# A fused cross-attention and expert kernel: weighted sums placed one step behind their scores

## The reference

```python
def attention(queries, keys, values):
    q = heads(queries @ Wq + bq); k = heads(keys @ Wk + bk); v = heads(values @ Wv + bv)
    scores = jnp.einsum('bhqd,bhkd->bhqk', q, k) / jnp.sqrt(jnp.float32(dh))
    attn = jax.nn.softmax(scores, axis=-1)
    ctx = jnp.einsum('bhqk,bhkd->bhqd', attn, v)
    return ctx.transpose(0, 2, 1, 3).reshape(B, L, D) @ Wo + bo

x = x + jnp.tanh(g_xattn[0]) * attention(_layernorm(x), ctx_1024, ctx_1024)
x = x + jnp.tanh(g_ffn[0]) * _moe(_layernorm(x))      # top 2 of 8 experts, relu between W1 and W2
```

## Time and profile before

| | us |
|---|---|
| median of 3 runs | 815.17 |
| lowest and highest run | 811.1 and 815.72 |
| the profiled execution | 809.99 |
| its span, first to last instruction | 807.8 |
| mean granted TensorE clock | 0.979 of full speed |

### The profile page before, as it was taken

How to read it: one execution, slowest core, us unless ns; L and a number is a source line. 1 busy time by engine, 2 the same in 40 slices (tenths; PEclk the granted TensorE clock), 3 DMA queues, 4 the chain that set the end, 5 groups by cost and what they waited for, 6 DMA issues and landing times.

```text
span 807.8 us, 21024 instructions
## 1 busy us (share of the span) xinstructions
PE 716.0 (89%) x6536; PEld 482.1 (60%) x6537; DVE 604.7 (75%) x1256; ACT 404.1 (50%) x783; POOL 460.3 (57%) x453
## 2 busy tenths in 40 slices
PE   3678999888887888877799999999999999999993
PEld 2344555454544445433477777777777777777771
DVE  5767888988889988887577877667666666776663
ACT  3266777677776776666533233333333333333330
POOL 6224544666566665544767767765565665655533
PEclk9799999999999999997999999999999999999997
DMA  6536655777677656653343323343323333222322
GB/s 185 135 107 196 198 160 181 173 183 191 140 188 187 172 135 188 161 158 100 87 110 49 53 48 50 52 56 46 46 47 52 53 46 47 46 49 41 53 34 27
DMA packets 96798, 85.45 MB, mean 106 GB/s; under 512 B 22256, under 2 KB 86000, under 8 KB 96592
## 3 DMA queue, kind: packets, MB, share of 16 engines
q1 hardware_dynamic: 80752, 65.73, 30.7%
q0 software_dynamic: 15680, 18.69, 14.9%
q10 hardware_dynamic: 288, 0.00, 0.0%
HBM read 53.61 MB, written 30.62 MB: 104 GB/s over the span
## 4 chain that ended last, share of the span: by engine, by line
PE 63%; DVE 19%; issue 9%; ACT 4%; DMA 2%; POOL 1%; another core or an unknown queue 1%; SPq 1%; DVEq 0%; POOLq 0%; ACTq 0%
PE banks L1779 22%; PE banks L1764 8%; PE banks L1766 7%; PE banks L1765 7%; DVE negmax L1127 6%; PE banks L1680 4%; PE banks L1590 3%; ACT probs L935 2%; PE banks L1668 2%; PE banks L1576 2%; PE banks L1750 2%; PE banks L1723 2%; DVE stats L1051 2%; PE banks L1640 1%; PE banks L1627 1%
## 5 line engine op out<-in xcount | busy, mean ns | idle before, releaser
L998 ACT ACTIVATE hid<-banks,b_col 128x256 f32<-128x256 f32 (+1 forms) x312 | 122.7, 453 | 200.9 <-DVE hl L1469 95.8
L1779 PE MATMUL banks<-wall,hh 128*128 x568 | 205.1, 381 | 2.6 <-DVE hl L1469 2.6
L787 POOL DMA_INDIRECT out_dram<-yb,dest_idx x71 | 125.5, 1767 | 121.1 <-DVE yb L1524 109.4
L1127 DVE TENSOR_REDUCE negmax<-banks 128x4 f32<-128x1024 f32 x128 | 155.6, 1217 | 21.1 <-PE banks L1640 20.8
L935 ACT ACTIVATE probs<-banks 128x1024 f32<-128x1024 f32 x128 | 130.9, 1024 | 69.0 <-PE banks L1668 66.0
L1764 PE MATMUL banks<-xh,wall 128*128 128x256 f16 (+1 forms) x624 | 161.3, 263 | 3.3 <-issue 2.4
L1765 PE MATMUL banks<-xl,wall 128*128 128x256 f16 (+1 forms) x624 | 161.2, 263 | 0.0
L1766 PE MATMUL banks<-xh,wall 128*128 128x256 f16 (+1 forms) x624 | 161.2, 263 | 0.0
L1779 PE MATMUL banks<-wall,hl 128*128 x568 | 144.9, 274 | 0.0
L1680 PE MATMUL banks<-probs,vaug 128*32 128x256 f32 x1024 | 83.6, 398 | 26.1 <-ACT probs L935 17.0
L709 POOL DMA_INDIRECT token_lists<-entry,place_i x64 | 69.4, 1084 | 61.1 <-ACT probs L935 41.3
(11 more groups left out here) (201 smaller groups left out, 1188.2 us busy)
## 6 DMA issues: line engine op xcount, KB each, us to landing
raw<-in_L_ffn_W SPq DMA_DIRECT2D x16, 512.0 KB, 6.3
wst<-in_L_ffn_W SPq DMA_DIRECT2D x16, 512.0 KB, 6.7
k_parts<-kparts SPq DMA_DIRECT2D x48, 128.0 KB
q_parts<-qparts SPq DMA_DIRECT2D x48, 128.0 KB
ks<-k_parts SPq DMA_DIRECT2D x64, 96.0 KB
qs<-q_parts SPq DMA_DIRECT2D x64, 96.0 KB
xin<-in_x SPq DMA_DIRECT2D x16, 256.0 KB, 2.8
cin<-in_ctx SPq DMA_DIRECT2D x16, 256.0 KB, 3.2
```

Of the source, the lines that this page charges most:

```text
L787: nc.gpsimd.indirect_dma_start(out_rows, bass.IndirectOffsetOnAxis(dest_idx[par][:, s:s + 1], 0), yb[par][:, s, :], None, compute_op=ALU.a ...
L998: ins = nc.scalar.activation(hid[half][:, c % (HC // 2), 0:subs(j) * P], banks[:, b, c % 2 * TS:c % 2 * TS + subs(j) * P], ACT.Relu, bias= ...
L1127: nc.vector.tensor_reduce(negmax[:, c, 8 * (g // 2):8 * (g // 2) + 8].rearrange("p (m g p2) -> p m g p2", m=2, g=2)[:, :, g % 2, :], banks ...
L1779: ins = nc.tensor.matmul(dst, h_[:, c, s * P:(s + 1) * P], w_, start=(c == 0 and k == 0), stop=(c == HC - 1 and k == 1))
```

## The change

On TensorE the weighted sum of step u-1 now stands in step u, behind that step's scores and maxima's scores. The weighted sum of step 7 stands in step 0 of the next body, behind its maxima's scores and ahead of the turned maxima, the k projection and the router. In the last body the weighted sums stay where they were, but for the eighth of batch 14, which comes there from the body before. On ScalarE the copy of the last group of sums moves with it, behind the first exponential of the next body. VectorE's, GpSimd's and SyncE's orders are the same.

```diff
-                def copy_out(g):
-                    n = m - 1
+                def copy_out(n, g):
                     act.wait_ge(av_mm, 8 * n + 2 * g + 2)
...
                         if v in (2, 4, 6):
-                            copy_out(v // 2 - 1)
+                            copy_out(m - 1, v // 2 - 1)
                     if v == 0:
+                        if post:
+                            copy_out(m - 2, 3)
                         if attention:
                             max_row(m - 1, 1)
...
-                if attention:
-                    copy_out(3)
+                if isinstance(m, int) and m == NB:
+                    copy_out(m - 1, 3)
...
                     if maxima:
                         scores_max(m, par, u)
+                    if u == 0 and post:
+                        attend(m - 2, par, 7)
+                    elif u > 0 and attention and not last:
+                        attend(m - 1, 1 - par, u - 1)
                     if u == 0:
                         if attention:
                             turn_max(m - 1, 1)
...
-                    if attention:
+                    if last:
                         attend(m - 1, 1 - par, u)
```

## The result

| | before | after |
|---|---|---|
| median, us (20 runs each) | 811.9 | 817.89 |
| lowest to highest | 808.52 to 815.72 | 814.2 to 821.29 |
| profiled execution: span, us | 807.8 | 815.8 |
| mean granted TensorE clock | 0.979 | 0.971 |

The ratio of after to before is 1.0068, with a 95% interval from 1.0054 to 1.0081: 0.7% or some 5.5 us slower, where 2.3 us faster was forecast. That is within 1%, but on the other side and clear of zero. The forecast counted from the three runs it was shown (815.17 us); over twenty runs the same kernel's median is 811.9, so the forecast gain would end at 809.6.

The account below looks back on a forecast made before the run. VectorE, 92% busy in mid-attention, was taken as the fuller engine, its router and maxima's-score waits the source of gain. Terms -0.5 - 1.4 - 0.2 + 0.15 - 0.35 = -2.3 us took 815.17 to 812.9; range 804 to 821.

Parts of the forecast that it names:

- The turns, in TensorE's queue: From one body to the next: eight turns gain 0.03 to 0.27 us each, four cost 0.21 to 0.31.
- The first bodies: Bodies 1 to 3, where VectorE truly waits for TensorE: gains of 0.5, 1.4 and 0.2 us.
- The waits: Before weighted sums near nothing; VectorE's for maxima's scores 11.7 to some 5 us, for the router 20.5 to some 25.
- the sum of the middle: Twelve turns of the attention part's long middle: gains of 0.93 against costs of 1.08, so it costs 0.15 us.
- the prediction's second kind of turn: Turns with a late reduction: turned maxima and logits come 0.31 us later; four such turns cost 1.08 together.
- The exponential's wait was the bound: Rival, TensorE's 21.7 us of waits before weighted sums: half back gives 804 us, nearly all 795; chance 0.15.
- The sum in the way at each turn: Rival, first step of a body: 0.57 us at 13 turns, net +5 us (820), or +11 (826); chance 0.20.
- The late gather: Rival, end of the attention part: GpSimd's late gather delays the experts, +3 us less 2.3, about 816; chance 0.05.
- Experts: Behind the attention part: they start 2 to 3 us sooner and keep their length.

Follow-up runs that it names:

- chip E: Fifth chip, one session: the changed kernel unedited, 0.9999 against the kernel before; with GpSimd's step 0 list scatter released one exponential later, 1.0016.
- chip A: One session: two versions with only part of the change, 1.0036 and 1.0024 against the kernel before; both kernels without list scatters, 798.51 before and 795.19 us after.
- the lag alone: Changed kernel with only weighted sums 1 to 7 moved, the eighth and ScalarE's last copy at the body's end as before: 1.0036 against the kernel before.
- eighth only: Kernel before with only the eighth weighted sum and its copy moved into the next body's first step: 1.0024 against the kernel before.
- chip D: One session: the changed kernel unedited, twice, 818.55 us (1.0079) and 815.97; with body 15 in the old order 1.0028; the kernel before 811.73 and 812.51 us.
- B: Chip, one session: changed kernel with step 0 scatter later 0.9980, eighth sum behind router 1.0024, weight loads later 1.0040; kernel before with scatter later 0.9964.
- end old: Changed kernel with body 15 in the old order, its weighted sums in their own steps: 1.0002 on chip C, 1.0028 on chip D, against the kernel before.

## Why the prediction was wrong

- **The turns, in TensorE's queue: right.** The router's logits started 3.48 to 3.56 us behind the reduction at the turns to bodies 4 to 6 (before 3.51 to 3.76), and 3.46 to 3.57 at every turn from there to body 14 on chip E.
- **The first bodies: right for body 2, too small behind it.** From body 2's second reduction to the logits behind it: 63.19 to 83.14 before, 63.02 to 81.47 after, 1.5 us less, forecast 1.4. From there to the end of body 6 another 0.8, where I had 0.2 and next to nothing. Body 1's 0.5 us can't be seen: its start scatters by more, since the end of body 2 lies between 77.7 and 81.6 us in profiles of the same order.
- **The waits.** In front of weighted sums 4.2 us are left: right. In front of maxima's scores they rose by 18.1 (14.8 to 32.9): right. VectorE's wait for these fell from 11.7 to 9.0, not to 5: too little. The router's waits rose to 30.5, not 25. With the waits in front of the same logits that the view names "issue", it is 22.9 us before (20.5 and 2.4), 32.2 after (30.5 and 1.7) and 25.0 on chip E (18.2 and 6.8): the rise was 2.1 us without late wakes, and 7.2 more with them. VectorE's share of the middle stretch fell to 89.8%, where I had over 90.
- **The step that failed** is the sum of the middle, "it costs 0.15", with its ground "no instruction and no DMA is added". It looked at TensorE's queue and left out GpSimd's, whose scatters are released by the exponentials that the change moves. At the turn to body 9 the second scatter was issued 3.01 us behind the reduction before (216.79 - 213.78) and 2.48 after (217.21 - 214.73), so that it stands 0.31 us behind the first, not 0.84, k's parts fall due 0.16 us behind its start, not 0.25 ahead of it, and the logits 0.95 us behind it, not 0.54. In bodies 8 and 10 the scatters keep their places, 0.3 us apart, but the logits fall due 0.3 us later against them, the very 0.31 us of the prediction's second kind of turn, and their lateness grows from 0.34 and 0.39 to 1.07 and 1.03 us. Whether the distance of the scatters or the moment of the wait decides isn't shown. In body 9 on chip E the third scatter came 7.77 us behind the reduction instead of 8.46, because the exponential that releases it came sooner, and share, at 8.11, ran into it and the residual sum; before, it slipped in ahead at 8.35. The two part versions on chip A show that this is the lag's doing: 1.96 us with the lag alone, 0.16 with the eighth sum alone. What this cost: share in every profile of the changed kernel itself, 1.5 us in each of bodies 7, 9 and 11 on E, of which bodies 8 and 10 gave 0.7 and 1.0 back, as onehot was caught for less; late wakes on some chips, in the first profile 1.0 us more in each of bodies 9 and 11, 1.9 in body 7, and 0.7 in bodies 8 and 10, and less on D (4.7 and 3.8 us in bodies 7 to 14 for 6.4).
- **Rivals.** "The exponential's wait was the bound": no; its waits went, and bodies 7 to 14 together gained nothing, not even on E (183.8 for 182.8). "The sum in the way at each turn": its size came out (+5 us) but neither its place nor its reason. "The late gather": GpSimd's index cast came at 384.44 us behind a wait of 7.89, 9 us later than before, and TensorE took up the gathered rows without idle time; no cost seen.
- **Experts.** They start 7.8 us later in the first profile (401.76 for 393.96) and keep their length there (414.1 for 413.9), as forecast. On chip E they start 2.05 us sooner (391.91), the figure that was forecast, but by luck: the middle costs 1.0 us there, body 15 takes 20.2 us for 22.5, and the twenty-three runs of the kernel before on that chip show no gain at all.

So of the 5.5 us, the late wakes carry the most, and the measured size depends on the chip or the session: on E the whole change is 0 (0.9973 to 1.0025), some 2 us worse than forecast, of which the exchange of share for onehot is 1.0 by the profile and the rest isn't placed. That signals come late in this way is shown; why they do stays open.

## What to carry to other kernels

A reordering on one engine moves the release times of all that is paced by it. List the indirect DMAs and the elementwise sums of GpSimd in the body, and check what VectorE and ScalarE wait for or run in the microseconds behind each, before and after the change; there a 0.2 us instruction can cost 2 us. When an effect is under 1%, run the unchanged pair on more than one chip: here the same change measured 1.0079 on one and 0.9999 on another, further apart than their intervals. And an experiment that is to explain an effect has to run where the effect is seen: the two part versions ran on a chip without late wakes, and so say nothing about them.

## What the runs showed of the hardware

- **Late wakes.** On chip D, on B where two scatters stood back to back, and in the first profile of the changed kernel, waits of VectorE and ScalarE that fell due within about 1 us of the start of the second scatter ended up to 2.0 us behind it, 0.7 to 1.8 us late. In five turns (bodies 7, 9 and 11 of the first profile, and one in each of two on D) k's parts and the logits started within 0.02 us of each other; elsewhere k's parts came 0.7 us or more sooner. In one profile each on A (eighth only), C (end old) and E (the changed kernel), with the scatters as close, the same logits started 0.04 us behind their matmuls. With 3 us between the scatters there were none of over 0.25 us in bodies 7 to 14 on B. The kernel before has them too: of 0.3 to 0.65 us there, and of 1.0 and 1.1 in body 15 (its first profile and chip D). By the trace's notes it is the update of the semaphore that comes late, 1.64 and 0.94 us at the turn shown. What in the chip holds it, and why chips differ, no run here tells; whether each chip is always of its kind isn't known beyond the profiles listed.
- **VectorE behind GpSimd.** Small SBUF-only instructions of VectorE (share, onehot, and the others of this arithmetic with two inputs) that start while GpSimd scatters, with the sum `xres` right behind, can be held until the sum is done: 0.16 us became up to 1.96. In the twenty profiles those that started up to 0.26 us behind the scatter's start kept their 0.2 us, and all that started 0.32 us or more behind it were held; reductions were not. Where no sum followed the scatter, share never took over 0.4 us. The rule in the Trainium skill, SBUF — State Buffer, section "SBUF: two separate sides", that the port pair shared by VectorE and GpSimd is an exclusive lock held for a whole instruction, fits: the trace agrees for `xres`, 1.28 us. That the wait began in the scatter ahead of it goes beyond one instruction. Reductions from PSUM next to a scatter or `xres` kept their 1.22 us.
- **TensorE's clock** fell to 1.2 GHz at the end of the attention part in all the profiles; in the kernel before, behind a stretch in which TensorE was busy for 6.81 of 10 us (360 to 370 us, clock 1.00; then 0.66). In the middle it fell in some executions and not in others of the same program: the changed kernel at 178 to 181 us in its first profile, at 226 to 229 on E, and in neither of the two on D.
